# A perceiver layer on one core: the scratch of projected queries laid out by pair of heads, channel and batch

## What is computed

```
q = layernorm(x) @ w_q                         # (32, 64, 16*64)
k, v = split(ctx @ w_kv)                       # (32, 1601, 16*64) each
scores = einsum('bhqd,bhkd->bhqk', q, k) / 8
out = softmax(scores) @ v                      # per head
x = x + out @ w_out + b_out
x = x + time_mixing(layernorm(x))              # decaying recurrence over 64 positions, sigmoid gate
x = x + relu(layernorm(x) @ w1 + b1) @ w2 + b2
```

## Time and profile before

| | |
|---|---|
| median of 3 runs | 2347.87 us (2347.65 to 2348.88) |
| the profiled execution's own time | 2348.63 us |
| its span, first to last instruction | 2346.8 us |
| TensorE busy | 2290.6 us (98% of the span) |
| VectorE, ScalarE, GpSimd busy | 1815.5, 1541.4, 1647.7 us |
| DMA packets, bytes | 410274, 438.97 MB |
| share of 16 DMA engines, queues of SyncE and ScalarE together | 79.2% |

### The profile page before, as it was taken

How to read it: one execution, slowest core, us unless ns; L and a number is a source line. 1 busy time by engine, 2 the same in 40 slices (tenths; PEclk the granted TensorE clock), 3 DMA queues, 4 the chain that set the end, 5 groups by cost and what they waited for, 6 DMA issues and landing times.

```text
span 2346.8 us, 43941 instructions
## 1 busy us (share of the span) xinstructions
PE 2290.6 (98%) x13696; PEld 2098.0 (89%) x13696; DVE 1815.5 (77%) x3664; ACT 1541.4 (66%) x2696; POOL 1647.7 (70%) x858
## 2 busy tenths in 40 slices
PE   7989999999999999999999999999999999899999
PEld 5769999999999999999999999999999998878788
DVE  7867777777777777777777777777777777789884
ACT  6756666666666666666666666666666666565444
POOL 4248888888888888888888888888888886421111
PEclk9999999999999999999999999999999999999999
DMA  8988888888888888888888888888888886987000
GB/s 228 261 222 197 195 191 199 199 199 199 199 198 199 200 199 200 199 200 199 200 199 201 199 200 199 199 200 200 200 200 199 200 197 157 212 202 197 1 10 28
DMA packets 410274, 438.97 MB, mean 187 GB/s; under 512 B 82529, under 2 KB 380897, under 8 KB 410209
## 3 DMA queue, kind: packets, MB, share of 16 engines
q1 hardware_dynamic: 391248, 425.66, 76.9%
q10 hardware_dynamic: 18960, 12.49, 2.3%
HBM read 167.42 MB, written 52.43 MB: 94 GB/s over the span
## 4 chain that ended last, share of the span: by engine, by line
PE 41%; POOL 31%; issue 17%; DVE 4%; SPq 3%; DMA 1%; ACT 1%; ACTq 0%; POOLq 0%; DVEq 0%
POOL p_pt_lo L667 17%; PE p_scores L1557 14%; PE p_acc L1577 9%; POOL p_nat L694 5%; PE p_acc L1579 4%; POOL p_q_lo L679 4%; POOL p_ct_lo L675 3%; POOL p_ct_hi L686 3%; SPq L462 2%; PE p_cols L1625 2%; PE p_scores L1683 2%; PE p_scores L1729 2%; PE p_cols L1716 2%; PE p_scores L1641 1%; PE p_scores L1507 1%
## 5 line engine op out<-in xcount | busy, mean ns | idle before, releaser
L667 POOL TENSOR_TENSOR p_pt_lo<-p_landed,p_pt_hi 128x768 fp32r<-128x768 f32 x504 | 991.0, 1987 | 326.3 <-ACT p_pt_hi L893 326.3
L1577 PE MATMUL p_acc<-p_nat,p_pt_hi 128*128 128x384 f32 x3024 | 890.4, 361 | 16.0 <-POOL p_pt_lo L667 14.8
L1579 PE MATMUL p_acc<-p_nat,p_pt_lo 128*128 128x192 f32 x3024 | 759.6, 251 | 0.0
L929 ACT ACTIVATE p_prob<-p_scores,p_negmax 128x800 f32<-128x800 f32 (+1 forms) x512 | 470.9, 925 | 382.5 <-DVE p_negmax L1266 382.5
L1557 PE MATMUL p_scores<-p_ct_hi,p_q_hi 128*128 128x512 f32 (+2 forms) x2048 | 703.0, 347 | 4.2 <-ACT p_prob L929 4.0
L1557 PE MATMUL p_scores<-p_ct_hi,p_q_lo 128*128 128x512 f32 (+2 forms) x2048 | 702.6, 346 | 0.0
L1577 PEld LDWEIGHTS p_acc<-p_nat,p_pt_hi 128*128 128x128 f32 x3024 | 569.3, 188 | 24.8 <-issue 14.1
L1579 PEld LDWEIGHTS p_acc<-p_nat,p_pt_lo 128*128 128x128 f32 x3024 | 578.8, 191 | 0.0
L893 ACT ACTIVATE p_pt_hi<-p_landed 128x768 fp32r<-128x768 f32 x504 | 398.6, 838 | 176.2 <-PE p_acc L1581 128.7
L1276 DVE STREAM_TRANSPOSE turned<-p_prob 128x1536 f32<-128x1536 f32 x256 | 452.6, 1768 | 0.0
L1557 PEld LDWEIGHTS p_scores<-p_ct_hi,p_q_hi 128*128 128x128 f32 x2048 | 388.4, 190 | 50.6 <-ACT p_prob L929 6.2
(11 more groups left out here) (253 smaller groups left out, 3128.6 us busy)
## 6 DMA issues: line engine op xcount, KB each, us to landing
p_landed<-turned SPq DMA_DIRECT2D x2032, 104.0 KB, 2.3
resid<-in_ctx SPq DMA_DIRECT2D x128, 288.0 KB, 5.0
o_scratch<-resid SPq DMA_DIRECT2D x256, 96.0 KB, 2.6
p_stage<-qk_scratch SPq DMA_DIRECT2D x31, 512.0 KB, 3.9
p_stage<-qk_scratch SPq DMA_DIRECT2D x62, 256.0 KB, 4.2
qk_scratch<-p_out_a SPq DMA_DIRECT2D x30, 512.0 KB, 5.3
p_stage<-in_ctxT SPq DMA_DIRECT2D x31, 401.0 KB, 4.7
p_stage<-in_ctxT SPq DMA_DIRECT2D x62, 200.5 KB, 5.6
```

The lines of the kernel that those rows point to most:

```text
L667: nc.gpsimd.tensor_tensor(pt_lo[:, t0:t1, :, :], by_tile(slot, t0, t1), bits(pt_hi[:, t0:t1, :, :]), ALU.subtract).then_inc(pt_lo_done, 1)
L929: nc.scalar.activation(prob[:, lo:hi], scores[:, S0 + lo:S0 + hi], ACT.Exp, bias=negmax[:, par:par + 1], accum_out=rowsum[:, par, h:h + 1] ...
L1577: nc.tensor.matmul(acc[k % 2][:, 0:2 * DC], pt_hi[:, t, :, :].rearrange("p i x -> p (i x)"), x[:, t, :], start=t == 0, stop=False, skip_gr ...
L1579: nc.tensor.matmul(acc[k % 2][:, 0:DC], pt_lo[:, t, :, :].rearrange("p i x -> p (i x)"), x[:, t, 0:DC], start=False, stop=False, skip_grou ...
```

## The change

The scratch of queries is laid out as `by_pair` has it. The store of a group writes, for each channel, the 8 batches in one run of 8 x 128 columns: 4096 B, where there were 8 runs of 512 B. The load of a batch reads, for each channel, 8 runs of 512 B (one for each pair of heads), where there was one of 4096 B. Bytes, number of DMAs, their places in the queues and the waits stay as they are.

```
-                dst = qk_dram[c * CB:(c + 1) * CB, rows, j * 2 * NQ:(j + 1) * 2 * NQ].rearrange("b c n -> c b n")
+                dst = by_pair(qk_dram)[j, rows, c * CB:(c + 1) * CB, :].rearrange("c b n -> c (b n)")
                 eng.dma_start(dst, buf[:, :, :, :].rearrange("p b h q -> p b (h q)"))...
...
             def load_qk(n, h, dst):
-                src = qk_dram[bass.ds(n, 1), :, :].rearrange("a c n -> (a c) n")
+                src = by_pair(qk_dram)[:, :, bass.ds(n, 1), :].rearrange("j c a n -> c j (a n)")
+                dst = dst.rearrange("p (j n) -> p j n", n=W)
                 if h == 0:
-                    sp.dma_start(dst, src[0:P, :]).then_inc(qk_in[0], 16)
+                    sp.dma_start(dst, src[0:P]).then_inc(qk_in[0], 16)
                 else:
-                    sp.dma_start(dst[0:DCB], src[P:DC, :]).then_inc(qk_in[1], 16)
-                    sp.dma_start(dst[DCB:P], src[P:DC, :]).then_inc(qk_in[1], 16)
+                    sp.dma_start(dst[0:DCB], src[P:DC]).then_inc(qk_in[1], 16)
+                    sp.dma_start(dst[DCB:P], src[P:DC]).then_inc(qk_in[1], 16)
...
-                    sp.dma_start(first_q[:, 0, :], qk_dram[0, 0:P, :]).then_inc(first_q_in, 16)
+                    src, dst = by_pair(qk_dram)[:, :, 0, :].rearrange("j c n -> c j n"), first_q.rearrange("p k (j n) -> p k j n", n=W)
+                    sp.dma_start(dst[:, 0], src[0:P]).then_inc(first_q_in, 16)
                     for half in (slice(0, DCB), slice(DCB, P)):
-                        sp.dma_start(first_q[half, 1, :], qk_dram[0, P:DC, :]).then_inc(first_q_in, 16)
+                        sp.dma_start(dst[half, 1], src[P:DC]).then_inc(first_q_in, 16)
```

More of the change, by code:

```diff
@@ L76, in odd_key, with by_pair @@
     return ctx_in[bass.ds(n, 1), NKV - 1:NKV, :].rearrange("a k c -> (a k c)").partition_broadcast(P)
-def by_pair(o_dram):
-    return o_dram.rearrange("b c n -> (b c n)").rearrange("(j c b n) -> j c b n", j=NH // 2, c=DC, b=NB)
+def by_pair(scratch):
+    return scratch.rearrange("b c n -> (b c n)").rearrange("(j c b n) -> j c b n", j=NH // 2, c=DC, b=NB)
 def identity(nc, pool, ident, ident_done):
@@ L381, in store_pair @@
             for buf, rows in zip(staged[g % SLOTS], (slice(0, P), slice(P, DC))):
-                dst = qk_dram[c * CB:(c + 1) * CB, rows, j * 2 * NQ:(j + 1) * 2 * NQ].rearrange("b c n -> c b n")
-                eng.dma_start(dst, buf[:, :, :, :].rearrange("p b h q -> p b (h q)")).then_inc(qk_stored[g % SLOTS], 16)
+                dst = by_pair(qk_dram)[j, rows, c * CB:(c + 1) * CB, :].rearrange("c b n -> c (b n)")
+                eng.dma_start(dst, buf[:, :, :, :].rearrange("p b h q -> p (b h q)")).then_inc(qk_stored[g % SLOTS], 16)
         def load_pair(eng, n):
```

## The result

The changed kernel takes 2353.93 us (median of 16 runs), the kernel before 2348.49 in the same session: ratio 1.0025, 95% interval 1.0018 to 1.0032. It is 5.4 us slower, where the forecast had 23. The profiled execution took 2354.5 us with a span of 2352.7, 5.9 longer than before.

A forecast was written before the change was run, and what follows sets the result against it. SyncE's queue time ahead of the third move was taken to bound stage 2, with TensorE never idle. 2348.63 + 31.5 (30 batches x 1.05) - 8.3 (stores' gain) = 2371.8, forecast 2371 us, range 2341 to 2400.

The forecast's parts named there:

- The bound: Stage 2: time that issues hold SyncE's queue ahead of the third move, not bytes, is paid one for one each batch.
- The zero slack: Stage 2: one step per batch is just on time or 0.3 us late, and TensorE has no idle time.
- The hold: Stage 2, behind the first query load's 1024 pieces: the second output store is held, +0.8 us a batch.
- the held move issue: Stage 2, behind the second and third query loads: the move's second issue is held 0.1 us a batch.
- The loads of stage 1: First queries and batch 1's load, 2048 pieces each: costed at nothing, since the queue waits for evacuations anyway.
- The longer issues: Stage 2: second and third query loads issue like stores of 512 pieces; +0.24 us by the row, 0.15 taken.
- The gain: Border of the stages and stage 1, from stores in fewer pieces: 5.8 + 1.5 + 1.0, 8.3 us in all.
- the clock: Border of the stages: with less idle time TensorE's clock may stay up, 1.5 us gained, bounds 0 and 3.4.
- The lower bound of the gain: Stores' gain at the border and in stage 1: at least 3 us, with 11 as upper bound.
- nothing is held in stage 2: Rival: query loads only issue longer, 3 to 7.5 us lost and 8.3 gained, 2343 to 2347 us; chance 0.17 (2340 to 2347).
- between: Case of 0.25 to 0.5 us lost a batch in stage 2, 2347 to 2355 us; chance 0.08.
- The loss of rate at large row pitches: Rival's ground, query reads in stage 2: pieces 16 KB and 3 MB apart read slowly, 2400 us and up; chance 0.06.

The follow-up runs named there:

- e1: Kernel before with a 256 B gap behind each 512 B, so loads have 512-byte pieces at short distances and stores keep theirs: 2362.39 us, ratio 1.0058.
- e8: Kernel before with the first 128-row load of a batch's queries issued as two loads of 64 rows, same 4096-byte pieces: 2373.77 us, ratio 1.0101.
- e4: Changed kernel with each batch's three query loads in the loop replaced by stores of the same pieces to spare scratch: 2387.37 us, ratio 1.0165.
- e9: Changed kernel with one pair of 64-row context loads issued from ScalarE's queue ahead of the third move, not from SyncE's: 2367.08 us, ratio 1.0070.
- e10: Kernel before with one pair of 64-row context loads issued from ScalarE's queue ahead of the third move: 2352.60 us, ratio 1.0018.
- e2: Changed kernel's stores kept, but query loads read 4096-byte runs from another input of the same shape: 2349.44 us, ratio 0.9997 to the kernel before.
- e12: Changed kernel with half of the raw context, and one pair of context loads issued by ScalarE ahead of the third move: 2335.36 us, ratio 0.9944.
- e13: Changed kernel, nothing left out, one pair of context loads issued from ScalarE's queue one step later, behind the third move's bytes: 2345.58 us, ratio 0.9984.
- e14: Kernel before with one pair of context loads issued from ScalarE's queue, its bytes behind the third move's: 2344.12 us, ratio 0.9978.

## Why the prediction came out too high

The direction was right; two terms were not, and both were too large. The loss was over by 21 us, the gain by 6, so part of the first error was cancelled by the second. That the sign came out right owes something to luck: the real loss of some 10 us against the forecast gain of 8.3, less the 2.7 given back at the end, would have left the two kernels level.

- **The bound.** That time in SyncE's queue ahead of the third move is paid one for one holds for every lengthening (changed, e1, e8, e4). "And not bytes" was only half true: the bytes issued ahead were the next limit just behind it, and took what was given back (e9, e10). The zero slack was right too: before the change the late move already cost about 0.2 us a batch.
- **The hold, where the forecast failed.** "The first output store goes in; the second would have ended near 83.7 and is held until 84.5: +0.8 us." It was carried over from stores in the full queues of stage 1 to loads in stage 2. Behind a load of 1024 pieces there nothing is held (2.02 us for the four), behind a store of them it is (2.60). With the held move issue, 0.9 of the 1.05 us a batch did not come. The loads of stage 1, costed at nothing, did hold a store by some 1.0 us (1.59 for 0.56), and it cost nothing to speak of: step 0 is 0.65 us early, in e2 0.80.
- **The longer issues**, put at 0.15, were 0.28 for the two 64-row loads and 0.03 for the first. The row for 512 pieces had given 0.24, and taking less than it was wrong. The loss came to 0.34 a batch, some 10 us in 30 batches, not 31.5.
- **The gain.** From the first move's start to its last issue are 11.3 us, 14.2 before and 9.7 in the forecast: one issue still took 1.64 us, right behind ScalarE's store at 142.31. The forecast end was right even so, since ScalarE's own store was next due: it took the data at 150.51 (forecast 150.3). Step 5 went ahead by 6.1 us beyond the 0.65 of stage 1 (forecast 5.8 and 1.5 for the clock, and 1.0). What was missing is who is next: the second move, which waits for the last query store to land. It gave back 4.8 us at once, and 2.0 were left at step 10. The clock's 1.5 us did not last: at step 5 the steps are 6.7 us ahead where ScalarE had started 5.6 ahead, but the lower level then fell behind the second move's wait, and in sum it was granted for 6.8 us in both kernels. The lower bound of the gain, 3, is below what its terms give (5.8 + 0 + 0), and no reason stands for it; the 2.0 that were left lie below both.
- **The rival "nothing is held in stage 2"** had the mechanism right and the end wrong: 2340 to 2347 rested on the gain of 8.3. With 0.34 a batch and 2 us of gain it would have given 2357 less what the last batches and stage 3 gave back (8.59 down to 5.9 between step 250 and the span's end), near the 2354 measured. The result lies in the case called "between", which had 0.08.
- **What the pages say.** The Trainium skill, "Perfetto Trace Analysis", section Per-instruction lifecycle, would have the issue's window cover its descriptors' generation, 96 us in all by the prediction's working. The trace disagrees: 1024 pieces issue in 0.39 us, 128 in 0.36. The loss of rate at large row pitches in "DMA: Bandwidth & Descriptors", section Latency and other measured facts, is neither confirmed nor refuted: the page's pitch is the one from partition to partition, which is 16 KB here, and the 3 MB lie between the pieces of one row. Loads of such pieces landed in 4.2 us, of whole rows in 3.9.

## What to carry to other kernels

A hold seen behind stores in one stage is no price for loads in another: cost each from a row of its own direction and of its own stage. Where a queue's end sets a landing, look at what bytes stand ahead of the same transfer before counting on shortening it; only when the issues ended earlier and fewer bytes stood ahead of the transfer (e12 to e14) did time come back. And a gain at a border is worth what the next waiter leaves of it, so follow the chain one wait further than the one removed.

## What the runs showed of the hardware

- In stage 2, 1024 query pieces of 512 B hold the issue after next when written to DRAM (0.95 us for 0.35) and not when read. In stage 1, with loads landing after some 8 us, reads of such pieces held a store's issue too (1.59 us for 0.56).
- A load whose source repeats its 64 rows with stride 0 in one issue takes 0.65 us to issue but still moves its 4096-byte packets at 11 a microsecond 3 to 13 us later; all 128 rows from one issue without the repeat land in 3.9. On average two of its packets were under way at once, some ten with two loads of 64 rows. It held later issues and cost 9 us a batch.
- A second queue added no room: a pair of 64-row loads moved to ScalarE's queue made a move on SyncE's land 1.3 us later behind its last issue (3.0 for 1.7) when its bytes fell ahead of or amid the move's.
- Small stores: the issue of a pair fell from 0.37 and 0.67 us to 0.33 and 0.47 with 128 and 64 pieces, in the changed kernel's line 383 between 28 and 56 us:

```profile
L383 SPq DMA_DIRECT2D qk_scratch<-p_out_a x9: 332/332/354, 28.4 to 55.5; - x9
L383 SPq DMA_DIRECT2D qk_scratch<-p_out_b x9: 472/472/530, 28.8 to 55.8; - x9
```
